# Attention scores and maxima on 32-row tiles of TensorE, one head's rows each, in a two-layer transformer kernel

## The reference

```python
scores = einsum('bhsk,bhtk->bhst', Q, K) / sqrt(head size)
attn = softmax(scores, axis=-1)          # over the 512 keys t
ao = einsum('bhst,bhtv->bhsv', attn, V)
```

## Time and profile before

| | |
|---|---|
| median of three runs | 543.95 us |
| span of the profiled execution | 541.2 us |
| TensorE matmul busy | 494.7 us (91%), 2782 instructions |
| VectorE busy | 315.8 us (58%) |
| ScalarE busy | 278.7 us (51%) |
| GpSimd busy | 136.3 us (25%) |
| mean granted TensorE clock | 0.978 |

### The profile page before, as it was taken

The page is one execution under the profiler, slowest core; times in us unless marked ns, Lnnn a source line. Parts: engine busy times, 40 slices in busy tenths (PEclk is TensorE's granted clock), DMA queues, the critical chain, the costliest instruction groups (busy, mean ns, idle before and its releaser), DMA issues.

```text
span 541.2 us, 7612 instructions
## 1 busy us (share of the span) xinstructions
PE 494.7 (91%) x2782; PEld 345.1 (64%) x2782; DVE 315.8 (58%) x826; ACT 278.7 (51%) x414; POOL 136.3 (25%) x136
## 2 busy tenths in 40 slices
PE   5899799998989999999999988999999999889980
PEld 4578678886545555554897865445555554669970
DVE  4654444567778787764263577877788663402223
ACT  6734344552546566667454653556656555205640
POOL 5755622331711101200000000101111005231551
PEclk9999899999999999999999998999999999899995
DMA  8970200000700000020000000000000002540003
GB/s 323 303 234 2 78 1 0 1 1 1 307 5 0 1 2 0 1 79 0 2 1 0 1 2 1 1 0 1 0 1 2 0 1 94 249 107 4 19 18 120
DMA packets 12868, 26.57 MB, mean 49 GB/s; under 512 B 1293, under 2 KB 10120, under 8 KB 11808
## 3 DMA queue, kind: packets, MB, share of 16 engines
q1 hardware_dynamic: 11392, 22.91, 12.5%
q0 software_dynamic: 1440, 3.18, 1.9%
HBM read 22.11 MB, written 5.26 MB: 51 GB/s over the span
## 4 chain that ended last, share of the span: by engine, by line
PE 77%; DVE 10%; ACT 5%; issue 3%; DMA 3%; POOL 2%; POOLq 0%; DVEq 0%; SPq 0%; ACTq 0%
PE PS L436 13%; PE PS L468 11%; PE PS L453 10%; PE PS L690 5%; PE PS L579 5%; PE PS L613 5%; PE PS L581 5%; PE PS L580 5%; PE PS L730 3%; PE PS L721 3%; DVE mx L1153 3%; PE PS L342 3%; PE PS L421 2%; PE PS L422 1%; PE PS L443 1%
## 5 line engine op out<-in xcount | busy, mean ns | idle before, releaser
L1153 DVE TENSOR_REDUCE mx<-PS 128x1 f32<-128x512 f32 x256 | 164.6, 685 | 41.8 <-PE PS L436 39.3
L854 ACT ACTIVATE wc_late<-PS 128x1024 f32<-128x1024 f32 x128 | 123.9, 1022 | 62.2 <-PE PS L453 62.0
L436 PE MATMUL PS<-Kp,Qs 128*128 128x512 f32 x256 | 95.9, 438 | 6.9 <-DVE mx L1153 5.2
L436 PEld LDWEIGHTS PS<-Kp,Qs 128*128 128x128 f32 x256 | 44.7, 190 | 70.4 <-DVE mx L1153 40.3
L453 PE MATMUL PS<-Qm,Kp 128*128 128x512 f32 x256 | 75.2, 415 | 0.8 <-DVE Qm L1165 0.6
L468 PE MATMUL PS<-wc_late,v_c 128*16 128x512 f32 x512 | 67.3, 598 | 0.7 <-ACT wc_late L854 0.7
L1438 POOL CAST Kp<-Ks 32x512 fp32r<-32x512 f32 x40 | 24.3, 607 | 135.0 <-ACT Ks L833 133.1
L453 PEld LDWEIGHTS PS<-Qm,Kp 128*128 128x128 f32 x256 | 46.5, 190 | 18.1 <-ACT wc_late L854 3.8
L579 PE MATMUL PS<-wc_late_r 128*128 128x512 f32 x96 | 41.7, 435 | 1.1 <-POOL xT_yT_r L1400 0.6
L1052 DVE TENSOR_SCALAR work<-PS,early 128x512 f32<-128x512 f32 x32 | 22.6, 747 | 25.1 <-PE PS L581 25.1
L954 ACT ACTIVATE work<-PS,late 128x160 f32<-128x160 f32 x64 | 19.8, 396 | 32.5 <-PE PS L721 32.5
(11 more groups left out here) (244 smaller groups left out, 743.5 us busy)
## 6 DMA issues: line engine op xcount, KB each, us to landing
wa<-wa_dram SPq DMA_DIRECT2D x8, 512.0 KB, 9.0
wa<-wc_dram SPq DMA_DIRECT2D x2, 2048.0 KB, 9.8
wc_late<-wc_dram SPq DMA_DIRECT2D x2, 2048.0 KB, 11.1
wb<-wb_dram SPq DMA_DIRECT2D x1, 2048.0 KB, 15.6
sel<-sel_dram POOLq DMA_DIRECT2D x2, 1024.0 KB, 5.6
late<-late_dram SPq DMA_DIRECT2D x1, 1572.0 KB, 14.9
packed_rows<-ao SPq DMA_DIRECT2D x1, 1290.0 KB, 22.9
wb<-packed_rows SPq DMA_DIRECT2D x5, 258.0 KB, 4.3
```

Of the source, the lines that this page charges most:

```text
L436: filled(mm(p, Qs[:, G % 3, qt * P:(qt + 1) * P], Kp[:, G % 3, j, :], start=True, stop=True), (L, "max", G, qt, j))
L854: A(E4[:, 2 * (i % 2) + jp, :, :], p, ACT.Exp, scale=float(HD[L]) ** -0.5).then_inc(taken[f"s{jp}"], 1)
L1153: V.reduce_max(mx[:, G % 2, qt, j:j + 1], p, AX.X).then_inc(taken[filled_at[key][0]], 1)
```

## The change

Each score and maxima matmul takes its head's 32 rows of `Ks` and of the queries alone, and names a 32-row tile of the array by the position of these rows (0, 32, 64, 96). Its result is the same, since the other 96 rows of Kp's copy were zero. `Kp` goes, `Ks` becomes float32r and three groups deep, and ScalarE writes it in one instruction for every group. With Kp go its zero fill, GpSimd's copies, their semaphore and TensorE's wait for it, and the stackK2 jobs. keep_warm reads `Ks[:, 0, :]`, all 128 rows. Nothing else moves.

```diff
-        Kp = sb("Kp", [P, 3, HPG, S], F32R)
-        Ks = sb("Ks", [P, 2, S])
+        Ks = sb("Ks", [P, 3, S], F32R)
...
-                return {0: [("stackK2", G + 2)] * (more and G > 0), 1: [("stackQ", G + 2)] * more,
-                        2: [("turn", G - 1)] * (G > 0),
+                return {0: [], 1: [("stackQ", G + 2)] * more, 2: [("turn", G - 1)] * (G > 0),
...
-                    if qt == 0 and G >= 3:
-
-                        pe.wait_ge(Kp_set, HPG * (L * KEYS + G - 3) + 2 * (half + 1))
                     for j in (2 * half, 2 * half + 1):
                         p = claim((L, "max", G, qt, j), slots[j % 2])
-                        filled(mm(p, Qs[:, G % 3, qt * P:(qt + 1) * P], Kp[:, G % 3, j, :], start=True, stop=True),
-                               (L, "max", G, qt, j))
+                        r = slice(SL * j, SL * (j + 1))
+                        filled(mm(p, Qs[r, G % 3, qt * P:(qt + 1) * P], Ks[r, G % 3, :], start=True, stop=True,
+                                  tile_position=(SL * j, 0)), (L, "max", G, qt, j))
...
                     for j in range(2):
-                        last = mm(p[:, j, :], Kp[:, G % 3, 2 * jp + j, kt * P:(kt + 1) * P], Qm[:, G % 2, :],
-                                  start=True, stop=True)
+                        r = slice(SL * (2 * jp + j), SL * (2 * jp + j + 1))
+                        last = mm(p[:, j, :], Ks[r, G % 3, kt * P:(kt + 1) * P], Qm[r, G % 2, :], start=True, stop=True,
+                                  tile_position=(SL * (2 * jp + j), 0))
...
-                def stackK(G, half):
-                    if G >= 3:
-
-                        if half == 0:
-                            p = wait_full(act, (L, "stack", G, 0))
-                            if L * KEYS + G > 4:
-                                act.wait_ge(Kp_set, HPG * (L * KEYS + max(G - 4, 0)))
-                            A(Ks[:, G % 2, :], p, ACT.Identity, bias=la("minus")).then_inc(taken["mi"], 1)
-                        return
+                def stackK(G):
                     p = wait_full(act, (L, "stack", G, 0))
-                    for j in (2 * half, 2 * half + 1):
-                        r = slice(SL * j, SL * (j + 1))
-                        last = A(Kp[r, G % 3, j, :], p[r, :], ACT.Identity, bias=la("minus")[r, :])
-                    if half:
-                        last.then_inc(taken["mi"], 1)
+                    A(Ks[:, G % 3, :], p, ACT.Identity, bias=la("minus")).then_inc(taken["mi"], 1)
...
-            nc.gpsimd.memset(Kp[:, :, :, :].rearrange("p a j s -> p (a j s)").bitcast(F32), 0.0)
...
-            def place_keys(L):
-
-                for G in range(3, NGB):
-                    wait_taken(pool, (L, "stack", G, 0))
-                    for j in range(HPG):
-                        rows = slice(SL * j, SL * (j + 1))
-                        nc.gpsimd.tensor_copy(Kp[rows, G % 3, j, :], Ks[rows, G % 2, :]).then_inc(Kp_set, 1)
-
-                        pool.wait_ge(Kp_set, HPG * (L * KEYS + G - 3) + j + 1)
...
-            place_keys(0)
...
-            place_keys(1)
```

More of the change, by code:

```diff
@@ L214, in build @@
         field_mx, field_exp = sem("field_mx"), sem("field_exp")
-        H_done, Kp_set, MP_ready, pv_read = sem("high_parts"), sem("Kp_set"), sem("maxima_placed"), sem("exps_used")
+        H_done, MP_ready, pv_read = sem("high_parts"), sem("maxima_placed"), sem("exps_used")
         coh_e, x_cond_set = sem("coh_expd"), sem("x_plus_cond")
@@ L256, in maxima_at @@
             return [divmod(h, 2) for h in (range(first, first + 1) if place == 0 else range(first + 1, first + n))]
-        KEYS = NGB - 3
         def jobs(L, i, place):
@@ L283, in build @@
         early_jobs = [{(8, 1): [("cT", 0)], (9, 0): [("qk", 0, 0)], (9, 1): [("v", 0)],
-                       (10, 0): [("stackK", 0), ("stackK2", 0)], (10, 1): [("stackQ", 0)],
-                       (12, 1): [("stackK", 1), ("stackK2", 1)], (13, 1): [("stackQ", 1)],
-                       (14, 1): [("stackK", 2), ("stackK2", 2), ("place", 0)],
+                       (10, 0): [("stackK", 0)], (10, 1): [("stackQ", 0)],
+                       (12, 1): [("stackK", 1)], (13, 1): [("stackQ", 1)],
+                       (14, 1): [("stackK", 2), ("place", 0)],
                        (15, 0): [("maxT", 0), ("max", TPB, 0)], (15, 1): [("max", TPB, 1)]},
                       {(8, 0): [("cT", 0)], (8, 1): [("qk", 0, 0)], (9, 0): [("qk", 0, 1)],
-                       (9, 1): [("stackK", 0), ("stackK2", 0)], (10, 1): [("stackQ", 0)], (11, 0): [("v", 0)],
-                       (11, 1): [("stackK", 1), ("stackK2", 1)], (12, 1): [("stackQ", 1)], (13, 0): [("tanh", 0)],
-                       (13, 1): [("stackK", 2), ("stackK2", 2)], (14, 1): [("place", 0), ("coh", 0)],
+                       (9, 1): [("stackK", 0)], (10, 1): [("stackQ", 0)], (11, 0): [("v", 0)],
+                       (11, 1): [("stackK", 1)], (12, 1): [("stackQ", 1)], (13, 0): [("tanh", 0)],
+                       (13, 1): [("stackK", 2)], (14, 1): [("place", 0), ("coh", 0)],
                        (15, 0): [("maxT", 0), ("max", TPB, 0)], (15, 1): [("max", TPB, 1)]}]
@@ L350, in keep_warm @@
                 for _ in range(n):
-                    mm(ps("m0"), Qs[:, 0, 0:P], Kp[:, 0, 0, :], start=True, stop=True)
+                    mm(ps("m0"), Qs[:, 0, 0:P], Ks[:, 0, :], start=True, stop=True)
             def field(step):
@@ L534, in job @@
                         maxima(*at)
-                    elif name not in ("stackK2", "place"):
+                    elif name != "place":
                         {"y": y_, "logits": logits, "count": count, "weightsT": lambda b: weightsT("b", b),
@@ L883, in job @@
                 def job(name, *at):
-                    if name in ("stackK", "stackK2"):
-                        stackK(at[0], int(name == "stackK2"))
+                    if name == "stackK":
+                        stackK(*at)
                     elif name in ("cT", "qk", "tanh", "coh", "stackQ", "aoT", "proj", "logits", "count"):
```

## The result

| | before | after |
|---|---|---|
| median | 543.99 us (543.36 to 546.19) | 572.25 us (565.28 to 581.39) |
| profiled execution, span | 541.2 us | 563.4 us |
| mean granted TensorE clock | 0.978 | 0.906 |

The ratio is 1.042 (95% interval 1.037 to 1.048): slower, on the far side of the range. The before column holds runs on the same chip as the changed kernel.

The account below looks back on a forecast made before the run. The prediction took VectorE's reductions, which free the two PSUM slots A1 waits for, to bound most loop steps. Its terms, 6.5 - 9.1 - 2.4 + 2.1 - 1.0 = -3.9, gave 540.0 us, range 531 to 552.

Parts of the forecast that it names:

- The bound: Attention loops: A1 waits for B1's reduction, so faster scores buy nothing there; plain steps stay at 3.29 us.
- Four row tiles at one time: Score matmuls: four start together and stream in 0.23 us instead of 0.93; full overlap with paid switches had chance 0.50.
- the serial loads: Rival: row-tile loads go one after another, scores start 0.11 us apart; +3.3, 547.3 us, chance 0.20.
- no overlap: Rival: row tiles run 0.23 us apart, every switch paid and nothing gained; +22, 566 us, chance 0.08.
- A switch costs 0.19: Each added change of tiling costs 0.19 us; 17 jobs between A1 and values per layer, +6.5 us in all.
- the free switch: Rival: switching to and from row tiles costs nothing for float32r; -19, 525 us, chance 0.06.
- The late steps: 13 loop steps with a longer job after half B, bound by TensorE: 0.54 us saved each.
- Halves between expert matmuls: Expert stages: a maxima half between full matmuls goes from 0.70 to 0.87 us over three intervals, +0.16 each.
- (4): Expert stages: 16 of 20 maxima halves count, +2.6 us, less 0.5 from ScalarE's single write of Ks.
- (5): Start of the second loop, clock at 0.50, VectorE waiting behind scores of 1.73 us: about -1.0 us.
- The tails: Last six steps of each layer, without maxima: 0.2 us saved a step, -1.2 per layer (0 to -2).
- the weight of the clock: Rival: more waiting and quarter rows drop the loops' clock to 0.50 in a third of steps; +26, 566 to 570, chance 0.10.

Follow-up runs that it names:

- scores_only: Only the score matmuls row-tiled, maxima on the full array, padded copies kept, against the kernel before: 540.38 us, 0.986; in five rounds 540.65 us, 0.988.
- t7_maxima: Only the maxima matmuls row-tiled, from step 7 of each loop on, scores on full rows, against the kernel before: 554.3 us, 1.012.
- t7_filler_full: Scores and maxima tiled from step 7 (base, 558.85 us), plus three unread 128-row matmuls ahead of the scores in steps 7 to 25: 554.25 us, 1.009 of the kernel before.

## Why the prediction was wrong

**What held, at full clock.**
- The bound. A plain step takes 3.28 us, 3.29 before, although its four scores take 0.34 instead of 0.93.
- Four row tiles at one time. In the step at 203.26, B0, B1 and two scores start within 0.01 us; the other two scores use the tiles of B0 and B1 and start 0.33 later. Both rivals without full overlap, the serial loads and no overlap, are out. But the four don't stream in the 0.23 of the prediction. In the step at 189.60 the four scores start within 0.01 us, and A0, next on the tile of the first of them, starts 0.34 behind it:

```profile
189.60 0.51 PE L448 MATMUL PS<-Qm,Ks 32*128 32x512 f32 x4
...
189.94 0.57 PE L430 MATMUL PS<-Ks,Qs 32*128 32x512 f32 x2
```

All 20 places of this trace where A0 follows four such scores at 1.00 have 0.34. The estimate of 0.30 that the prediction worked out from the Trainium skill (TensorE: Matmul & The Clock Gate, Part 3) is nearer to this than 0.23 is. It moves little here, since the scores are mostly not on the path.
- A switch costs 0.19. Forecast for a stackQ step 3.95, measured 3.94; a step with turn went from 3.69 to 3.87. This rules out the free switch.
- The late steps, in part. A step of 4.38 went to 4.03, which is 0.54 saved and 0.19 paid. It is the first step of rows 6: there A1 loaded 0.56 behind the reduction, and now 0.05 behind it, at 190.01. In the second loop some stay late: a step of 4.36 became 4.30.

```profile
188.67 1.29 DVE L1136 TENSOR_REDUCE mx<-PS 128x1 f32<-128x512 f32 x2 [1.38 <-PE PS L430]
...
189.71 0.48 PEld L430 LDWEIGHTS PS<-Ks,Qs 32*128 32x128 f32 x2
```

- Halves between expert matmuls, 0.87 forecast. The chain of the changed kernel, where rows 12 had 0.47:

```profile
106.59 0.42 PE PS L430
107.02 0.44 PE PS L574
```

0.42 and 0.44 are 0.86. All of the stages outside the loops together became 1.2 us longer, where (4) and (5) of the sum together had 2.1 - 1.0 = 1.1. That tests neither the 16 halves nor the -1.0: the fall at the start of the second loop was 3.4 us long before and 10.2 us after.
- The tails. Forecast -1.2 in each layer, measured -1.9 and -0.6. In rows 9 ScalarE's 1.94 a pair seemed to cap the step at some 1.94; single steps went down to 1.56 and 1.42, with longer ones between them. The values' loads of one such step:

```profile
253.81 0.13 PEld L463 LDWEIGHTS PS<-wc_late,v_c 128*16 128x16 f32 x8
...
255.37 0.13 PEld L463 LDWEIGHTS PS<-wc_late,v_c 128*16 128x16 f32 x8 [0.24 <-issue]
```

**The total without the clock.** I compared each step at half clock with the same kind at 1.00 (in this trace, or in those with a full-row start): 13.3 us too long in the first loop and 12.8 in the second. 563.4 - 26.1 = 537.3. The forecast was 541.2 - 3.9 = 537.3. That the two agree to the tenth is luck. Without the clock the first loop became 2.3 us shorter where the terms give 1.1, the second 2.9 where they give 4.0, and most of the first steps of a loop have no tiled step at 1.00 to be set against, so for them the comparison counts neither savings nor switches. Two sums of the prediction also don't come out of the terms beside them, the 2.1 for the small lateness of stackK steps (they give 1.9) and the -19 for the free switch (about -17.5); neither moves the result.

**The step that failed** is the weight of the clock. The prediction named it as a rival with the right place and price: 1.5 us a step (measured 1.6 for a plain step, 1.9 for a stackQ step), a third of the steps, +26 us (measured 26.1), "about 566 to 570". The profiled run took 565.3 and the median 572. It got a chance of 0.10 and was left out of the range, because rows 1 show 1.00 throughout both loops and the fall in rows 13, just ahead of the second loop, followed on a wait. The sum itself went by 1.00 in every step. The rival named two causes, more waiting and a quarter of the rows, and the runs put the fall on the second. But in the loops of before nearly every matmul names 128 rows, so rows 1 said nothing on what fewer rows do. A condition that the change alters in nearly every instruction, and that the trace of before holds fixed, is not bounded by that trace. The range should have reached to 572.

**Why it falls** is shown in part. Shown: it is the tiles and not the copies, not the switches alone, not waiting; with one tile only, at 99% busy, the clock falls with the rows named, 0.98, 0.90 and 0.79. Shown too: full-row matmuls beside the tiles keep the clock, or most of it: maxima (scores_only, under 1 us at 0.50 in the loops), scores (t7_maxima, 7) or unread ones (t7_filler_full, 14, against 41 in its base). What stays open: why tiled maxima alone fall at the starts of the loops (tiled scores don't), and what moves the falls from run to run. The medians of one program on two occasions differed by 11 us, and the changed kernel's own runs range over 18. Argued only: in the changed kernel the overlap packs more rows into the time of one matmul, which would be why it stands at 0.91 and not at the 0.79 of the single tile on 32 rows. Its steps are shorter too, and no run separates the two. Nor does a run separate the rows that a matmul names from the size of the tile, which change together.

## What to carry to other kernels

Zero-padded operands on the full array aren't only waste: here they kept TensorE at 2.4 GHz, and taking them out in both kinds of matmul lost 4%. Taking them out in the scores alone gained 1.2%, in the maxima alone it lost 3.8%, so which kind is tiled matters as well. Try row tiles for part of a loop's matmuls, keep the others on 128 rows, and compare the granted clock by window before the lengths of steps. When a change alters how much of the array nearly every matmul uses, let the range reach to the half-clock case, whatever the clock of before; and first ask whether the engine is on the path at all, since a matmul beside VectorE's reductions is worth nothing at any speed.

## What the hardware showed that was not expected

- In these runs the granted clock went with the rows that the matmuls name, not with how long TensorE is busy and not with whether those rows hold zeros: 0.98, 0.90 and 0.79 for 128, 64 and 32 rows without overlap, at busy shares of 98 to 99% in the stretches shown.
- Tiles on different rows, each with 128 columns to load, start 0.01 us apart or less, as 203.26 and 203.27 above show, where full matmuls are 0.235 apart. Four of them in flight hold their tiles for 0.34 us (189.60 to 189.94), about one and a half times as long as one full matmul.
- VectorE's first two small operations had taken 3.03 and 2.89 us beside GpSimd's zero fill and ended within 0.1 us of it. Without the fill each takes 0.23. The fill and the first operation before, and the first operation after:

```profile
1.27 5.22 POOL L1387 MEMSET Kp<- 128x6144 f32 x1
3.54 3.03 DVE L1012 CAST ident_r<-early 128x128 fp32r<-128x128 f32 x1 [3.54 <-DMA early<-early_dram]
...
3.61 0.23 DVE L995 CAST ident_r<-early 128x128 fp32r<-128x128 f32 x1 [3.61 <-DMA early<-early_dram]
```

It is off the path. A small operation of VectorE can thus last until the end of an instruction of GpSimd that no semaphore ties it to.
